# Setup of a two-layer attention and expert kernel: bias regrouping, end waits and table clearing rearranged

## The reference

```python
qkv = x @ Wqkv + bqkv                      # 16 heads of 16 features
scores = q . shifted k for 40 offsets (0..32, 48, 64, 96, 128, 192, 256, 384), * scale
scores = scores + pos_bias.T               # one bias per offset and head
out = softmax(scores) weighted sum of the shifted v
x = layernorm(x + (out * sigmoid(x @ Wgate + bgate)) @ Wout + bout)
logits = relu(x @ rw1 + rb1) @ rw2 + rb2   # top 2 of 8 experts, 1024 slots each
disp[expert, position] += x                # unused slots stay zero
y = relu(disp @ ew1 + eb1) @ ew2 + eb2     # per expert, gathered back, weighted
x = layernorm(x + y)
```

## Time and profile before

| | us |
|---|---|
| median of 3 runs | 1871.81 |
| lowest and highest of them | 1871.53, 1876.36 |
| the profiled execution, its own time | 1871.79 |
| the span of its trace | 1870.0 |
| setup, from the start to the first cast of x | 50.6 |
| busy in the span: PE, DVE, ACT, POOL | 1385.5, 970.6, 904.0, 699.1 |

### The profile page before, as it was taken

How to read it: one execution, slowest core, us unless ns; L and a number is a source line. 1 busy time by engine, 2 the same in 40 slices (tenths; PEclk the granted TensorE clock), 3 DMA queues, 4 the chain that set the end, 5 groups by cost and what they waited for, 6 DMA issues and landing times. The chain is left out here.

```text
span 1870.0 us, 72122 instructions
## 1 busy us (share of the span) xinstructions
PE 1385.5 (74%) x31232; PEld 879.1 (47%) x31232; DVE 970.6 (52%) x2122; ACT 904.0 (48%) x1552; POOL 699.1 (37%) x652
## 2 busy tenths in 40 slices
PE   0566787867877687777778767787663899999970
PEld 0234454544454454444445444445432466667750
DVE  3315466555555565555546655655662455555425
ACT  2243364544645355443636544463543656665526
POOL 2221343433435254333526433352433023332245
PEclk9765686777768686777768776777666899999995
DMA  9473352624334262524335242523401534444238
GB/s 209 92 197 67 100 120 80 153 71 119 86 97 108 75 149 76 129 68 108 79 94 129 82 112 60 128 65 95 98 4 50 148 91 93 97 93 104 55 35 359
DMA packets 195691, 195.21 MB, mean 104 GB/s; under 512 B 62847, under 2 KB 179663, under 8 KB 192160
## 3 DMA queue, kind: packets, MB, share of 16 engines
q1 hardware_dynamic: 177872, 167.18, 34.0%
q0 software_dynamic: 15360, 15.10, 5.1%
q10 hardware_dynamic: 2176, 8.52, 2.0%
HBM read 115.37 MB, written 86.25 MB: 108 GB/s over the span
## 5 line engine op out<-in xcount | busy, mean ns | idle before, releaser
L409 POOL TENSOR_TENSOR p<-p 128x512 f16<-128x512 f32 x96 | 129.4, 1348 | 283.2 <-ACT p L812 283.1
L832 ACT COPY featT<-gp 128x1024 f16<-128x1024 f16 x96 | 92.5, 1013 | 260.3 <-PE gp L557 260.3
L564 PE MATMUL gp<-featT,wr 128*128 128x512 f16 x768 | 194.3, 411 | 23.0 <-DVE mT L981 17.0
L1129 POOL DMA_INDIRECT disp<-y,sidx x128 | 179.1, 1399 | 52.3 <-issue 37.9
L409 DVE TENSOR_TENSOR p<-p 128x512 f16<-128x512 f32 x96 | 85.1, 886 | 199.9 <-ACT p L812 199.4
L1407 POOL DMA_INDIRECT xln<-y,place x64 | 105.0, 1640 | 218.1 <-DVE y L1549 177.3
L1445 PE MATMUL up<-rowsT,w 128*128 128x512 f16 x768 | 172.9, 386 | 9.3 <-DVE w L1522 5.3
L1459 PE MATMUL dn<-w,h 128*128 128x256 f16 x1536 | 170.1, 273 | 0.0
L1459 PEld LDWEIGHTS dn<-w,h 128*128 128x128 f16 x1536 | 149.7, 98 | 17.3
L811 ACT ACTIVATE p<-st 128x512 f16<-128x512 f32 x192 | 116.3, 606 | 81.6 <-PE st L609 41.5
L1506 ACT ACTIVATE h<-up,b 128x512 f16<-128x512 f32 x128 | 88.1, 689 | 129.9 <-PE up L1445 71.7
(11 more groups left out here) (174 smaller groups left out, 2793.8 us busy)
## 6 DMA issues: line engine op xcount, KB each, us to landing
v_near<-v_dram SPq DMA_DIRECT2D x32, 528.0 KB, 7.7
qk_dram<-qk SPq DMA_DIRECT2D x64, 256.0 KB, 3.8
o_dram<-o_far SPq DMA_DIRECT2D x64, 136.0 KB, 3.1
o_back<-o_dram SPq DMA_DIRECT2D x16, 544.0 KB, 4.0
v_dram<-vs SPq DMA_DIRECT2D x16, 528.0 KB
v_far<-v_dram SPq DMA_DIRECT2D x64, 132.0 KB
disp<-y ACTq DMA_DIRECT2D x8, 1040.0 KB, 22.9
rows<-disp SPq DMA_DIRECT2D x16, 520.0 KB, 3.5
```

Of the source, the lines that this page charges most:

```text
L409: engine.tensor_tensor(p16[:, b, 1, :], p32[:, b, :], p16[:, b, 0, :], ALU.subtract).then_inc(is_split, 1)
L564: last = nc.tensor.matmul(dst, lhs(a, c), rhs(b, c), start=(k == 0), stop=(k == len(todo) - 1))
L832: gp_done(nc.scalar.copy(featT[:, i, :, :].rearrange("f c t -> f (c t)"), bank[:, :].bitcast(F16)), n, stage, PART_OF_T[stage], i)
L1129: nc.gpsimd.indirect_dma_start(out=disp[:, :], out_offset=bass.IndirectOffsetOnAxis(ap=sidx[:, t, k:k + 1], axis=0), in_=y16[n.par][:, t, ...
```

## The change

- `bqk_dram` and its five transfers go. SP loads `bqkv[0:512]` as one row on all 128 partitions (128 descriptors of 2 KB). DVE multiplies four permuted pieces of it by the identity matrix, sums along the row, and scales two of four columns.
- The load of `pos_bias` moves from SP to the head of ACT's program. The four loads of `rb2` become one.
- DVE builds the bias vectors ahead of the weight splits, with 16 copies instead of 80. One of its two fills of `ks` moves to POOL.
- SP no longer waits in `setup` for the vector stores, but ahead of the table loads. ACT no longer waits for the biases; ACT, DVE and POOL each wait for `biases_in` ahead of their first use in `attention`. The wait for `pad_in` moves to the first load of `v_near`.
- ACT issues two clearing transfers in setup instead of six, three in iteration -1 in slot 7, and one each in iteration 0 in slots 9, 11 and 13. None stands in slot 15 of iteration -1 any more.

```diff
-CLEARED_IN_SETUP = 6
+CLEARED_IN_SETUP = 2
+CLEAR_AT = {(-1, 7): (2, 3, 4), (0, 9): (5,), (0, 11): (6,), (0, 13): (7,)}
...
+                    if n.i is None and n.c == 0:
+                        sp.wait_ge(pad_in, 32)
...
-            sp.wait_ge(pad_in, 32)
             sync.dma_start(xln[TOK:TOK + SPARE, :], g["x_rows"][0:SPARE, :]).then_inc(spare_in, 16)
+            sp.wait_ge(vectors_stored, 64)
             load_tables()
...
-                if it.i is None and it.c == -1 and k == H - 1:
+                if it.i is None and (it.c, k) in CLEAR_AT:
                     act.wait_ge(rest_in[0], 64)
-                    for c in range(CLEARED_IN_SETUP, CLEARINGS):
+                    for c in CLEAR_AT[it.c, k]:
                         clear_slots(nc.scalar, disp, y16[0], c).then_inc(cleared, 16)
...
             dve.wait_ge(tables_in, 256)
+            dve.wait_ge(biases_in, 80)
...
-                sp.dma_start(*loads[5], allow_slow_non_contiguous=True).then_inc(here[5], 16)
-                for u in range(4):
-                    src = g["bqkv"][D * (u // 2):D * (u // 2 + 1)].rearrange("(p e d) -> e d p", e=2, d=HD)[u % 2]
-                    sp.dma_start(g["bqk_dram"][u].rearrange("(d p) -> d p", p=PAIRS), src, allow_slow_non_contiguous=True).then_inc(regrouped, 16)
+                sp.dma_start(qk_bias, g["bqkv"][0:2 * D].partition_broadcast(P)).then_inc(qk_bias_in, 16)
                 for dst, src in loads[6:]:
...
-                sp.wait_ge(regrouped, 64)
-                sp.dma_start(a["bqk"][:, :], g["bqk_dram"].rearrange("u f -> f u"), allow_slow_non_contiguous=True).then_inc(loaded, 16)
                 sp.wait_ge(vec_done, 1)
...
-                sp.wait_ge(stored, 64)
...
+                nc.gpsimd.memset(a["ks"][1][:, :, :].rearrange("p a t -> p (a t)").bitcast(FP32), TWO_ONES)
...
+                nc.scalar.dma_start(*loads[5], allow_slow_non_contiguous=True).then_inc(here[5], 16)
...
-                act.wait_ge(loaded, 16 * (len(loads) - 5))
-                nc.scalar.mul(a["bqk"][:, 0:2], a["bqk"][:, 0:2], HD ** -0.5)
...
+                dve.wait_ge(qk_bias_in, 16)
+                dve.wait_ge(identity, 1)
+                for u in range(4):
+                    row = qk_bias[:, D * (u // 2):D * (u // 2 + 1)].rearrange("f (p e d) -> f e d p", e=2, d=HD)[:, u % 2]
+                    nc.vector.tensor_tensor(picked[:, u, :].rearrange("f (d p) -> f d p", p=PAIRS), row,
+                                            ident[:, :].rearrange("f (d p) -> f d p", p=PAIRS), ALU.mult).then_inc(bias_step, 1)
+                dve.wait_ge(bias_step, 4)
+                nc.vector.tensor_reduce(a["bqk"][:, :], picked, AX.X, ALU.add).then_inc(bias_step, 1)
+                dve.wait_ge(bias_step, 5)
+                nc.vector.tensor_scalar(a["bqk"][:, 0:2], a["bqk"][:, 0:2], HD ** -0.5, None, ALU.mult)
```

More of the change, by code:

```diff
@@ L233, in build @@
     qk_dram = [dram(f"qk_dram{i}", (2, 2, 2, P, N), F16) for i in range(2)]
-    bqk_dram = dram("bqk_dram", (4, P), FP32)
     m_dram = [dram(f"m_dram{i}", (H, N), F16) for i in range(2)]
@@ L347, in attention @@
         x_loaded, cleared = sem("x_loaded"), sem("cleared")
+        biases_in, vectors_stored = sem("biases_in"), sem("vectors_stored")
         setup(nc, g, locals())
@@ L899, in rout @@
                             act.wait_ge(qk_split, n.at(4, 12) if n.i is not None else min(n.at(4, 12), 4 * B))
+                        if ht == 0 and n.i is None and n.c == 0:
+                            act.wait_ge(biases_in, 80)
                         if ht == 0 and (n.i is not None or n.c > 0):
@@ L1103, in outp @@
                     pool.wait_ge(xres_loaded, n.at(16, 16))
+                    if n.i is None and n.c == 0:
+                        pool.wait_ge(biases_in, 80)
                     nc.gpsimd.tensor_tensor(xres[:, :, :], xres[:, :, :], g_bo, ALU.add).then_inc(xres_ready, 1)
@@ L1176, in setup @@
                   (r2_s, a["wr2"][:, :, 0:E], a["wr2"][:, :, E:2 * E])]
-        loaded, stored, regrouped = sem("setup_loaded"), sem("setup_stored"), sem("setup_regrouped")
+        qk_bias_in, identity, bias_step = sem("qk_bias_in"), sem("identity"), sem("bias_step")
+        qk_bias = flat(a["p32"])[:, 3 * 512:4 * 512]
+        picked = a["o_back"][:, :, :, :].rearrange("p t h c -> p (t h c)")[:, 0:4 * P].rearrange("p (u f) -> p u f", f=P)
         hi, lo = sem("setup_hi"), sem("setup_lo")
@@ L1188, in setup @@
                  (a["bo"][:, :], g["bout"].partition_broadcast(P)),
-                 (a["br1"][:, :], g["rb1"].rearrange("(u p) -> p u", p=P))] + \
-                [(a["br2"][:, t, :], g["rb2"].partition_broadcast(P)) for t in range(TILES)]
+                 (a["br1"][:, :], g["rb1"].rearrange("(u p) -> p u", p=P)),
+                 (a["br2"][:, :, :], bass.AP(g["rb2"].tensor, 0, [[0, P], [0, TILES], [1, E]]))]
         with nc.Block() as block:
@@ L1226, in _ @@
                 nc.gpsimd.affine_select(out=ident[:, :], in_=ident[:, :], compare_op=ALU.not_equal, fill=1.0,
-                                        base=0, pattern=[[-1, P]], channel_multiplier=1)
+                                        base=0, pattern=[[-1, P]], channel_multiplier=1).then_inc(identity, 1)
                 nc.gpsimd.affine_select(out=a["before_mat"][:, :], in_=a["before_mat"][:, :], compare_op=ALU.is_gt, fill=0.0,
@@ L1259, in _ @@
                 nc.scalar.copy(wide, zero_rows[:, :, :].rearrange("p t d -> p (t d)").bitcast(FP32)[:, 0:704].unsqueeze(1).to_broadcast([P, 6, 704]))
-                act.wait_ge(loaded, 16 * (len(loads) - 5))
-                nc.scalar.mul(a["bqk"][:, 0:2], a["bqk"][:, 0:2], HD ** -0.5)
             @block.vector
             def _(dve):
-                for i in range(2):
-                    nc.vector.memset(a["ks"][i][:, :, :].rearrange("p a t -> p (a t)").bitcast(FP32), TWO_ONES)
                 for v in (vec_n[0], vec_f[0]):
@@ L1271, in _ @@
                 last.then_inc(vec_base, 1)
+                nc.vector.memset(a["ks"][0][:, :, :].rearrange("p a t -> p (a t)").bitcast(FP32), TWO_ONES)
                 def split(k):
@@ L1276, in split @@
                     nc.vector.scalar_tensor_tensor(l, src, WS, h, ALU.mult, ALU.subtract).then_inc(lo, 1)
-                for k in range(11):
-                    split(k)
                 dve.wait_ge(here[5], 16)
@@ L1284, in _ @@
                 dve.wait_ge(vec_base, 3)
[L1285 to L1288, removed]
-                last.then_inc(vec_done, 1)
+                for i in range(2):
+                    nc.vector.tensor_copy(vec_n[i][:, 63 - NEAR:64], pb_16[i][:, NEAR::-1])
+                    for k, off in enumerate(OFFSETS):
+                        if off > NEAR:
+                            z = 31 - off // FAR_STEP
+                            last = nc.vector.tensor_copy(vec_f[i][:, z:z + 1], pb_16[i][:, k:k + 1])
+                last.then_inc(vec_done, 1)
+                for k in range(11):
+                    split(k)
+                dve.wait_ge(qk_bias_in, 16)
[8 more added lines that the diff above has]
+                nc.vector.tensor_scalar(a["bqk"][:, 0:2], a["bqk"][:, 0:2], HD ** -0.5, None, ALU.mult)
                 for k in range(11, len(splits)):
```

4 lines of the change are left out of this document (2 added, 2 removed).

## The result

The changed kernel took 1853.14 us, median of 4 runs (1846.0 to 1860.93), against 1871.67 for the kernel before (4 runs, 1869.69 to 1876.36): ratio 0.990, 95% interval 0.985 to 0.994. Two later series, on other chips, each beside the kernel before, gave 0.987 (0.983 to 0.991) and 0.990 (0.987 to 0.994). By these ratios the three gains are 18 to 24 us, some 20; the medians differ by 15 to 24. Setup alone gained 29.4 in the trace. So about a third of it is given back.

What follows compares the result with a forecast made beforehand. Setup was taken as bound by transfers, SP's queue held up by single-number writes to `bqk_dram`. Terms -28.0 - 1.9 + 1.5 + 0.4 gave -28.0 from 1871.8, so 1843.8 us, range 1837 to 1857.

Steps and rivals of the forecast that it cites:

- The stall: In setup, single numbers written to `bqk_dram` hold the DMA engines for 16.5 us; the change has no such writes.
- The start of the batches: End of setup: the batches begin at about 22.6 us instead of 50.61.
- the first term: SP in setup: shorter issues and no wait for the stores' landing gain 28.0 us, bounds 21 and 33.5.
- Rival B: Setup: vector stores have room at once, DVE or ACT ends setup at about 17 to 19; time 1839, chance 0.18.
- The first batch: SP's way to the first store of queries: the waits exchanged cost nothing, 0.5 us either way.
- The three clears in iteration -1: Iteration -1, in a DMA hole from 80 to 92 us: cost 0; without the hole up to 8.5 us.
- the second single clear: Iteration 0 slot 11, at about 155 us, in a DMA hole from 145 to 162: cost 0.
- The two clears gone from slot 15: Iteration -1: batch 1's queries' store lands sooner, on the path to `o_back`; gain 1.9 us, bounds 0 and 2.5.
- the clear before `o_back`: Iteration 0 slot 9, across the stores and the load of `o_back`: cost 1.5 us, bounds 0 and 2.8.
- The distance from m0 to the first merge: From the first `m_dram` store to the first `ob` merge: 47.05 us, to change by under 2.
- rival D: First iterations give back some of setup's gain, clears delaying `o_back` and the queries' store no earlier; time 1856, chance 0.10.
- My own test: Forecast wrong if the first cast is past 30 us or the first merge over 3 us later against the cast.

Runs made afterwards that it cites:

- e_regroup: The kernel before with only the query and key bias regrouped on chip: no transfers to `bqk_dram`, six clears and end waits of setup kept; ratio 0.993.
- e_clears: The kernel before with only the clears moved to where the change puts them, the writes to `bqk_dram` kept; ratio 0.999.
- e_all_setup: The changed kernel with all eight clears in setup and none in a batch; ratio 0.995.
- e_old_clears: The changed kernel with the clears where they were: six in setup, two in iteration -1 slot 15; ratio 0.991.
- e_old_clears_end: The changed kernel with six clears in setup, two in iteration -1 slot 15, and setup's end wait for the vector stores kept; ratio 0.993.
- e_place: The changed kernel with iteration -1's three clears right behind the first cast of x, and iteration 0 slot 11's clear in iteration 1 slot 3; ratio 0.992.
- e_four: The changed kernel with four clears in setup, two in iteration -1 slot 15, one each in iteration 1 slots 3 and 4; ratio 0.991.
- e_keep_end: The changed kernel with setup's end wait for the vector stores kept; ratio 0.991.

## Why the prediction was right, and where it was off

**The stall** was read rightly. That single numbers written to `bqk_dram` held the engines, and not the clears or the row loads, is now shown from both sides by `e_regroup` and `e_clears`. What in them does it, the 4 B, the one small piece of DRAM or the way from DRAM to DRAM, no run separates. The argument that carried was the landing of the fourth transfer at the end of the second slow stretch.

**The start of the batches** was put at 22.6 and was 21.2 to 22.1; the gain of the first term, 28.0, was 29.4 in the first trace and 27.8 over the mean of two before and three after. Its pieces were off against each other: the row loads took 0.45 to 1.75 and not 1.27 each, the vector stores 8.59 in all and not 10.1, but the load of x took 3.15 instead of 1.94 to issue. Rival B, that DVE or ACT would end setup, did not happen: SP did, ACT waited 4.16 us at the common end.

**The first batch**, put at nothing within 0.5, cost about that bound: the first store of queries stands 12.45, 11.42 and 11.94 us behind the cast, against 11.30 and 11.56 before, 0.5 on the means. The step missed that the padding stores would find the queue full of vector stores, which the old end wait had let drain.

**The three clears in iteration -1**, put at 0, are the step that failed. They cost 3.3 us of PE's time, 3.62 against 0.28 (3.66 against 0.38 on the means). The row on which I relied, DMA share 0.01 from 80 to 92, is right; the reasoning from it was not. It looked for data transfers that would wait, and left out that PE's own program comes by the same engines. The hole was also wrong for the second single clear: 145 to 162 was put at 0, and PE's wait there grew from 1.59 and 2.14 to 3.52, 4.05 and 4.07, 2.0 on the means. In all, from the cast to m0 the loss is 3.7 on the means (46.5 against 42.8), from m0 to m2 3.1 (146.4 against 143.3), where I had the sum at 0. The first is the stop and the 0.5; of the second only the 2.0 is tied to a cause.

**The two clears gone from slot 15** were to gain 1.9, and **the clear before `o_back`** to cost 1.5. The distance from m0 to the first merge was to change by under 2, and there the forecast held: 47.4, 46.9 and 46.9 against 47.05 and 46.8, with DVE's wait for `o_back` 11.92 against 11.93. The two terms can't be parted in these two kernels. A third kernel hints at both: `e_all_setup`, with neither on that way, has 45.1, the kernels with the pair in slot 15 (the kernel before, `e_regroup`, `e_old_clears`, `e_old_clears_end`) 46.4 to 47.7. So each may cost some 1.3 to 2.6 us there, and they cancel; that is one trace of the kernel without them. At m2 nothing of the pair is left to see: `e_regroup`, which keeps it, has the shortest way from m0 to m2 of all, 138.7, and `e_all_setup`, which has none in a batch, 138.9.

The forecast of 1843.8 is 9 us under the measured median, of which about 7 are those two losses and the rest is within what runs of one kernel differ by. The range, 1837 to 1857, held the time through rival D, whose mechanism (queries' way to `o_back`) was a different one. The gain of setup was forecast for the right reason; that the time fell in the range in spite of the stops is luck. My own test, that the first merge may not come over 3 us later against the cast, failed: 94.4 against 89.3.

A rule of the Trainium skill had been set against the row: "DMA: Bandwidth & Descriptors", section "Queues, rings and completion order", has an engine take some 9 to 17 descriptors from one queue at a turn. Equal counts alone, 1534 and 1692 packets in `e_regroup`, 396 and 396 in the earlier trace rows, would come of such turns too. But in the kernel before, in every stretch of 0.17 us from 31 to 34, SP's queue passes 11 to 18 packets and ACT's 12 to 19, about one each for an engine and never a gap. So the measurement decides for one each. The same page, section "Specifications", says that below 512 B the DMA engines do a read-modify-write. No run here separates that, but it can't be the whole of the stall: in `e_regroup` vector stores of 192 B a row were issued among the clears at 401 GB/s. Only the numbers of 4 B, all to one 2 KB, stalled.

## What to carry to other kernels

When a DMA issue takes many us, look at the queue's packets and at GB/s against the busy share: here a full share with a fifth to an eighth of the bandwidth came from four bad transfers, and the landing time of the last named them. A stretch without data transfers is not free for bulk transfers if an engine there runs many small instructions: its program comes by the same DMA engines. Beside long instructions bulk did less harm (`e_place`, `e_four`), but not ahead of small loads that someone waits for. Before crediting an early start, follow it to the next store that every version must do; here 4 us of start were 2 at the first store of the queries and 0 at m0, since the clears of the same change took the 2 back.

## What the hardware showed that was not expected

Program loads of 16 KB on a queue of their own, 4.0 us apart without clears, came 7.0 to 7.5 us apart where three clears ran beside them, and PE went on 2.2 to 2.5 us behind the load in every trace looked at. PE so stood still 3.5 to 4.1 us at a fixed point of its program, in batch 0 and in batch 1 alike (once, in `e_keep_end`, 1.85), against 0.2 to 0.5 and 1.6 to 2.1 without clears there. 512 single numbers of 4 B written to 2 KB of DRAM held all 16 engines at 48 to 85 GB/s for 16.5 us, where the same clears ran at 401 GB/s without them. And one kernel's steady part of 1060 us differed by up to 15.5 us from trace to trace, more than most of these edits are worth.
